# Scores of an attention layer for two heads at a time, in a four-layer graph network kernel

## The reference

```python
Q = (x @ Wq + bq).reshape(b, n, N_HEADS, HEAD_DIM)      # 4 heads of 64
K = (x @ Wk + bk).reshape(b, n, N_HEADS, HEAD_DIM)
V = (x @ Wv + bv).reshape(b, n, N_HEADS, HEAD_DIM)
scores = jnp.einsum('bnhd,bmhd->bhnm', Q, K) * scale
scores = jnp.where(mask, -jnp.inf, scores)
attn = jax.nn.softmax(scores, axis=-1)
out = jnp.einsum('bhnm,bmhd->bnhd', attn, V).reshape(b, n, OUT_F)
out = out @ Wo + bo                                      # then a layernorm with gamma, beta
```

## Time and profile before

| | us |
|---|---|
| median of 3 runs | 5317.18 |
| lowest and highest run | 5315.99, 5329.2 |
| the profiled execution, first to last instruction | 5314.2 |
| PE busy in it | 4239.7 (80%) |
| DVE, ACT, POOL busy in it | 2645.0 (50%), 1096.3 (21%), 691.8 (13%) |
| mean granted TensorE clock, 1 being 2.4 GHz | 0.848 |

### The profile page before, as it was taken

How to read it: one execution, slowest core, us unless ns; L and a number is a source line. 1 busy time by engine, 2 the same in 40 slices (tenths; PEclk the granted TensorE clock), 3 DMA queues, 4 the chain that set the end, 5 groups by cost and what they waited for, 6 DMA issues and landing times.

```text
span 5314.2 us, 60410 instructions
## 1 busy us (share of the span) xinstructions
PE 4239.7 (80%) x23394; PEld 3424.6 (64%) x23394; DVE 2645.0 (50%) x6555; ACT 1096.3 (21%) x2256; POOL 691.8 (13%) x789
## 2 busy tenths in 40 slices
PE   5877878778787787878878788787887878878787
PEld 4666666666666676656766567666676566765667
DVE  3554545545455454455544555444554545545454
ACT  1211212112121121311213112131211312212122
POOL 1111010110101101011010110111101111111111
PEclk8988879888898888978889788897888988888888
DMA  2000000000000000000000000000000000000000
GB/s 50 1 9 8 1 17 1 9 8 1 17 1 9 8 1 17 1 9 8 1 17 1 9 9 1 17 1 9 8 1 17 1 9 9 2 16 1 9 1 9
DMA packets 38382, 42.44 MB, mean 8 GB/s; under 512 B 2480, under 2 KB 37296, under 8 KB 38064
## 3 DMA queue, kind: packets, MB, share of 16 engines
q1 hardware_dynamic: 37552, 36.97, 2.1%
q0 software_dynamic: 512, 1.05, 0.2%
HBM read 21.24 MB, written 16.78 MB: 7 GB/s over the span
## 4 chain that ended last, share of the span: by engine, by line
PE 70%; DVE 14%; ACT 6%; issue 5%; POOL 5%; SPq 0%; DMA 0%; DVEq 0%; POOLq 0%; ACTq 0%
PE ps L817 19%; PE ps L898 8%; PE ps L759 7%; PE ps L751 6%; PE ps L852 5%; PE ps L772 5%; PE ps L881 5%; PE ps L783 4%; PE ps L840 4%; PE ps L743 4%; ACT prob L351 3%; POOL prob L301 3%; DVE stats L484 3%; DVE hn L495 2%; PE ps L806 2%
## 5 line engine op out<-in xcount | busy, mean ns | idle before, releaser
L817 PE MATMUL ps<-vals,probT 128*128 128x65 f32 x8192 | 1127.8, 309 | 19.5 <-DVE probT L564 19.5
L817 PEld LDWEIGHTS ps<-vals,probT 128*128 128x128 f32 x8192 | 1123.0, 226 | 29.9 <-DVE probT L564 29.9
L743 PE MATMUL ps<-ident,hn 128*128 128x128 f32 x1024 | 235.5, 420 | 807.4 <-DVE hn L495 807.4
L743 PEld LDWEIGHTS ps<-ident,hn 128*128 128x128 f32 x1024 | 199.4, 222 | 837.3 <-DVE hn L495 831.0
L564 DVE SCALAR_TENSOR_TENSOR probT<-ps,gval,adjT 128x512 f32<-128x512 f32 x1024 | 690.6, 742 | 52.4 <-PE ps L806 52.4
L351 ACT ACTIVATE prob<-prob,negmax 128x512 f32<-128x512 f32 x640 | 452.6, 713 | 580.1 <-DVE negmax L620 352.0
L537 DVE COPY probT<-ps 128x512 f32<-128x512 f32 x320 | 207.6, 687 | 558.3 <-PE ps L772 558.3
L898 PE MATMUL ps<-vals,probT 128*128 128x64 f32 x4096 | 478.5, 273 | 0.0
L898 PEld LDWEIGHTS ps<-vals,probT 128*128 128x128 f32 x4096 | 472.5, 192 | 0.0
L881 PE MATMUL ps<-kT,qT 64*128 64x512 f32 x1024 | 436.0, 598 | 5.7 <-DVE vals L647 5.7
L772 PE MATMUL ps<-ident,prob 128*128 128x128 f32 x2560 | 368.1, 288 | 74.2 <-ACT prob L351 52.4
(11 more groups left out here) (103 smaller groups left out, 4826.5 us busy)
## 6 DMA issues: line engine op xcount, KB each, us to landing
x_in<-in_x SPq DMA_DIRECT2D x32, 512.0 KB, 3.4
out_x<-x_out SPq DMA_DIRECT2D x32, 512.0 KB, 3.0
probT<-in_adj SPq DMA_DIRECT2D x1, 1024.0 KB, 5.4
probT<-in_L_gnn_W SPq DMA_DIRECT2D x2, 256.0 KB, 6.3
a_bc<-in_L_gnn_a POOLq DMA_DIRECT2D x8, 64.0 KB, 12.0
w<-in_L_gnn_W SPq DMA_DIRECT2D x1, 256.0 KB, 9.3
wgat<-in_L_gnn_W SPq DMA_DIRECT2D x1, 256.0 KB, 11.4
wgat<-in_L_gnn_W SPq DMA_DIRECT2D x2, 128.0 KB, 15.5
```

What stands on the lines that cost most here:

```text
L743: last = nc.tensor.transpose(ps[s][:, k, t * P:(t + 1) * P], hn[s][:, t, k * P:(k + 1) * P], ident[:, :])
L817: last = nc.tensor.matmul(ps[s][:, h % 2, t * DV:(t + 1) * DV], probT[s][:, h % 2, j, t * P:(t + 1) * P], vals[s][:, j, h * DV:(h + 1) * D ...
```

## The change

Only layer 2's order and its use of two banks change; no arithmetic is added or removed.

- PE computes the scores of both heads of a pair together: for each t and stream, head h on partitions 0 to 63 into bank 0, and right behind it head h + 1 on partitions 64 to 127 into bank 1. A bank holds one head, so a stream has one bank for each head, and the pair for t waits until both mask steps of t - 1 of that stream are done.
- PE then does the tail of h, then the tail of h + 1, and only then the scores of the next pair. No scores are left to do beside a tail.
- DVE does the 16 mask steps of a pair in a row, and one `negmax` for each stream for both heads.
- ACT's order is now: eight exponentials of h, then the copies of h with the exponentials of h + 1 between them, then the copies of h + 1.

The core of the diff (`score()` numbers the scores in their new order; the waits of `masked_max` follow it):

```diff
+        def score(layer, h, t):
+
+            return t if layer == 0 else NT + (h // 2 * NT + t) * 2 + h % 2
...
-                for h in range(-1, H):
-                    if h >= 0:
-                        for t in range(0, NT, 2):
-                            for s in streams:
+                for h in range(0, H, 2):
+                    for t in range(NT):
+                        for s in streams:
+                            exponentials(i, s, 2, h, t)
+                    for t in range(NT):
+                        for s in streams:
+                            if t % 2 == 0:
                                 weights_out(i, s, 2, h, t)
-                    if h + 1 < H:
-                        for t in range(NT):
-                            for s in streams:
-                                exponentials(i, s, 2, h + 1, t)
+                        for s in streams:
+                            exponentials(i, s, 2, h + 1, t)
+                    for t in range(0, NT, 2):
+                        for s in streams:
+                            weights_out(i, s, 2, h + 1, t)
...
-                bank = (2 + t) % 4 if layer == 0 else t % 2
+                bank = (2 + t) % 4 if layer == 0 else h % 2
...
-                for h in range(-1, H):
-                    if h + 1 < H:
+                for h in range(H):
+                    if h % 2 == 0:
                         for t in range(NT):
                             for s in streams:
+                                masked_max(i, s, 2, h, t)
                                 masked_max(i, s, 2, h + 1, t)
                         for s in streams:
-                            masked.wait(dve, s, i, att(2, h + 2, 0))
-                            nc.vector.tensor_scalar(negmax[s][:, h + 1, :], rowmax[s][:, h + 1, :],
+                            masked.wait(dve, s, i, score(2, h + 2, 0))
+                            nc.vector.tensor_scalar(negmax[s][:, h:h + 2, :], rowmax[s][:, h:h + 2, :],
                                                     -QK_SCALE, None, ALU.mult).then_inc(shift_ready[s], 1)
                     if h >= 0:
...
-                for h in range(-1, H):
-                    if h + 1 < H:
-                        g = h + 1
-                        at = slice((g % 2) * D, (g % 2 + 1) * D)
+                for h in range(H):
+                    if h % 2 == 0:
                         for t in range(NT):
                             for s in streams:
-                                if g == 0 and t == 0:
+                                if h == 0 and t == 0:
                                     kT_ready.wait(pe, s, i, 1)
                                     val_ready.wait(pe, s, i, 2)
-                                elif g or t >= 2:
-
-                                    masked.wait(pe, s, i, att(2, g, t) - 1)
-                                nc.tensor.matmul(ps[s][:, t % 2, :], qT[s][at, g // 2, t * P:(t + 1) * P],
-                                                 kT[s][at, g // 2, :], start=True,
-                                                 stop=True).then_inc(e_ready[s], 1)
+                                else:
+
+                                    masked.wait(pe, s, i, score(2, h, t))
+                                for g in (h, h + 1):
+                                    at = slice((g % 2) * D, (g % 2 + 1) * D)
+                                    nc.tensor.matmul(ps[s][:, g % 2, :], qT[s][at, h // 2, t * P:(t + 1) * P],
+                                                     kT[s][at, h // 2, :], start=True,
+                                                     stop=True).then_inc(e_ready[s], 1)
                     if h >= 0:
                         for t in range(NT + 1):
                             for s in streams:
```

More of the change, by code:

```diff
@@ L156, in gnn_stack_kernel @@
         shift_a = Signal("shift_a", 1)
-        shift_ready = Signal("shift_ready", 1 + H)
+        shift_ready = Signal("shift_ready", 1 + H // 2)
         lrelu_ready = Signal("lrelu_ready", NT)
@@ L342, in exponentials @@
             def exponentials(i, s, layer, h, t):
-                a = att(layer, h, t)
                 buf = h % 2
@@ L349, in exponentials @@
                 if t == 0:
-                    shift_ready.wait(act, s, i, 1 if layer == 0 else h + 2)
+                    shift_ready.wait(act, s, i, 1 if layer == 0 else h // 2 + 2)
                 nc.scalar.activation(prob[s][:, buf, t, :], prob[s][:, buf, t, :], ACT.Exp,
@@ L520, in masked_max @@
             def masked_max(i, s, layer, h, t):
-                a = att(layer, h, t)
+                a = score(layer, h, t)
                 buf = h % 2
-                bank = (2 + t) % 4 if layer == 0 else t % 2
+                bank = (2 + t) % 4 if layer == 0 else h % 2
                 mask = mask_pos if layer == 0 else mask_nz
```

## The result

The changed kernel takes 5344.83 us (median of 6 runs, 5333.8 to 5376.93) against 5317.06 us before: a ratio of 1.006, 95% interval 1.0034 to 1.0086. The profiled execution's own time is 5352.4 us, its span 5350.6.

The account below looks back on a forecast made before the run. PE was taken to bound the kernel (busy 80% of the span). Span 5314.2 + 93 (layer 2 waits) + 166 (clock lost) = 5573, plus 3 for the median: 5575 us, 4.9% slower; range 5450 to 5780.

Parts of the forecast that it names:

- what bounds layer 2: Layer 2: PE's stream paces it; after the change DVE's mask steps pace scores, and PE waits for ACT's copy.
- the +93 us of my sum: Layer 2 at full clock: two pairs of 39.2 us make 78.4 against 72.58, +5.8 us a step.
- One reading under it: Where head 0's scores meet head 1's: 10 passes in 2.10 us against 9 in 3.40, 0.21 against 0.38 us each.
- the clock in layer 2: Layer 2's first tails: clock falls after each pair's hole, 5.2 us a pair, +10.4 us a step, +166 us.
- Rival 1: Layer 2: clock stays low through the whole first tail, 11 us a pair, about 5760 us; chance 0.20.
- Rival 2: Layer 2 scores: the two heads' passes do not overlap in a long row, +109 us, 5685 us; chance 0.08.
- rival 3: Layer 2: the clock does not fall, or costs nothing, 5410 us; chance 0.10.
- rival 4: Layer 2: faster, the halved score passes come out whole, 14.1 us a step saved, 5091 us; chance 0.03.
- the sentence on the other layers: Other layers: range holds shifted clock effects; a 65-column row beginning at 0.50 is worth 6.5 us, two places a step.
- the two terms of layer 2: Layer 2: added waits at full clock, +93 us, and loss of clock in the first tails, +166 us.
- the best of my rivals: The faster case, rival 4: layer 2's halved score passes come out whole, 5091 us; chance 0.03.

Follow-up runs that it names:

- e7: Changed kernel with idle transposes filling PE's waits ahead of the 65-column passes (layers 1, 3) and ahead of each first tail (layer 2): 5185.23 us, ratio 0.9745.
- e5: Kernel before with idle transposes filling PE's short waits in layers 1 and 3, including the 1.51 us one ahead of the 65-column passes: 5093.74 us, ratio 0.957.
- e10: As e7, but ACT's first copy of a pair behind four exponentials, not eight, and 9 fillers, not 34, in the second hole: 5089.82 us, ratio 0.9569.
- e4: Changed kernel with only ACT's order altered, the first copy of a pair behind four exponentials in place of eight: 5487.88 us, ratio 1.0316.
- e6: Changed kernel with the same fillers as e5, in layers 1 and 3 alone: 5332.06 us, ratio 1.0018.
- e3: Kernel before, shifted by 0.9 us a step with 8 more idle transposes ahead of layer 2's first scores: 5306.26 us, ratio 0.998.
- e2: Changed kernel with 18 idle transposes in each of layers 1 and 3, the 1.51 us wait left open: 5419.02 us, ratio 1.0193.
- e11: Changed kernel, shifted by 0.9 us a step with 8 more idle transposes ahead of layer 2's first scores: 5443.87 us, ratio 1.0231.
- e1: Kernel before with 18 idle transposes in each of layers 1 and 3, the 1.51 us wait left open: 5272.06 us, ratio 0.9926.

## Why the prediction was wrong

**Right: what bounds layer 2.** The halves overlap (eight passes in 2.35 us), DVE paces the scores (a round of four in 2.65 to 2.68 us against 2.61 forecast), PE waits 4.04 us for the copy behind the eighth exponential (I said some 4), and e7 measures the stage at full clock by itself: 78.7 us a step against my 78.4, the +93 us of my sum being 91.5 between e5 and e7 (5185.23 - 5093.74). One reading under it was wrong, without harm: in the windows of the earlier trace rows, 10 and 9 are the passes that ran in them; 8 began in either, so in 0.26 us each and not 0.21 where the heads meet.

**Right, and a little too large: the clock in layer 2.** Forecast +10.4 us a step, measured 8.2 (86.97 less 78.74). It stayed low for different lengths in the two pairs, 13.08 and 15.60 us in the step shown, a loss of 3.2 and 5.7. Rival 1 (low to the end of the first tail) held in neither. The Trainium skill's rule behind this rival (TensorE: Matmul & The Clock Gate, Part 4: PE-mode transpose), that transposes do not count for the clock, has e7 against it, for float32 transposes: there nothing but transposes fills the holes, and the clock is 1.00 from the first score to the last aggregation pass. What I had set against the rival myself, that transposes alone bring the clock back, was picked from one place of two: sixteen transposes right ahead of the 64 slow passes of the earlier trace rows ran at 0.50 for 3.66 us (2293.44 to 2297.10), and the clock stayed there through the passes. Rival 2 (no overlap) is refuted, rival 3 too (0.84 over the stage), and rival 4: even with ACT's copy earlier and the clock held, attention takes 73.1 us (e10) against 72.6.

**The step that failed** is the sentence on the other layers: "It also holds what the shifted times do to the clock in the other layers: whether a row of 65-column passes begins at 0.50 is worth 6.5 us each time, and there are two such places in a step." I had named the mechanism, but put its mean at nothing, without looking how the kernel before stood, and took it for held by the range. By my own figures it was not: 2 x 6.5 x 16 = 208 us, while the range ended 125 us under 5575.

What the runs showed in its place: in the kernel before, three of four such places (two steps, layers 1 and 3) already ran slow, 74.4 us a step where the floor is 60.3 (e5). So there were 14.0 us a step to win; had every row taken the 43.2 us of the slowest, there would have been 12.0 to lose. The change won 13.5, almost all, 217 us of the 230 that layer 2 lost. That it fell out so is not to the idea's credit: e4 has the same order and won 0.2.

The condition and the size were off too. A row that begins at 0.50 costs 7.5 us, and the dearer ones, 13.0, begin at 1.00: there the clock falls 2.2 us into the row and stays down for 27.25. Put into the sum with what e5 measures as the floor, 5573 - 16 x 14.0 would have been some 5350 us. That this would lie so near is in part luck: the two terms of layer 2 were 29 us too high (93 + 166 against 230), and 22 us outside the rows stood nowhere.

**What stays open.** That the low clock in the 65-column passes comes of PE's idleness ahead of them is shown (e5, e6: filled, they are fast in every step of both orders), and that a shift changes which rows are slow when it is not filled (e3). Why the changed order's moments come out well in nearly every step, and those of layer 3 in e4 badly in every one, I did not derive. It also means that the 0.6% is no property of the idea: kernels with this order, and layer 2's holes left open, stand between 5332 and 5488 us (e2, e4, e6, e11 and the change).

## What to carry to other kernels

Where PE's clock falls in a kernel's waits, a change's effect in its own stage can be worked out from rows, but its effect on the whole cannot, until each later stage that runs partly at the low clock is listed with what it takes at either level: those that are slow now are chances of the change, those that are fast its risks. To compare two orders, fill PE's waits with idle work in both first; here that turned 0.6% into 4.7% with the waits of layers 1 and 3 filled (e6 against e5) and into 1.8% with those of layer 2 filled as well (e7 against e5), and a 2.7% loss (e4 against the change) into a gain of 1.8% (e10 against e7). And the filler itself was worth more (4.3%, with short waits alone) than the reordering could have been by the best of my rivals (5091 us, 4.2%).

## What the runs showed of the hardware

- Of the waits filled in e5 and e6, none was longer than 1.51 us. Left open, that one stands ahead of all 32 rows of e1; in 11 of them, all in layer 3, the clock fell 2.6 us behind the start of the row, although PE had been busy since.
- The clock can stay at 1.2 GHz while PE is busy without a pause: 27.25 us in the windows above (650.85 to 678.10), with 65-column passes and two groups of eight transposes.
- Matmuls on the two halves of the array's rows (partitions 0 to 63 and 64 to 127) overlap in float32 too: PE's busy time for the same 1024 score passes went from 436.0 to 284.7 us (e5 and e7), though each pass lasted 637 ns in place of 598.
- The change's own runs lie between 5333.8 us, at a mean clock of 0.855, and 5376.93 us, at 0.846; those of e7 lie within 1.9 us of each other (5183.65 to 5185.49).
